# Gated cross-attention kernel: a third stack buffer, whole stacks loaded at once, one merge transfer, a reordered sync queue, and value products of 512 queries in every second slot

## The reference

```python
q, k, v = proj(Wq, bq, norm(x)), proj(Wk, bk, c), proj(Wv, bv, c)   # each 128 x 512
q, k = rope(q, 8), rope(k, 8)                                       # on half of the 16 channels
p = softmax(einsum('bhqd,bhkd->bhqk', q, k) / sqrt(16))             # 8 heads, 512 x 512
x = x + tanh(g_xattn) * (Wo @ einsum('bhqk,bhkd->bhqd', p, v) + bo)
y = (silu(gate) * up) @ w_down ; x = x + tanh(g_ffn) * y / rms(y)   # gate, up = norm(x) @ w_gu
```

## Time and profile before

| what | us |
|---|---|
| median of 3 runs | 921.22 (918.21 to 933.62) |
| the profiled execution | 918.37 |
| its span | 916.6, so 1.8 lie around it |
| mean granted TensorE clock | 0.945 of full speed |
| busy: TensorE, VectorE, ScalarE, GpSimd | 815.8 (89%), 522.1, 483.6, 178.5 |
| first score of batch 0; of batch 1 (step 0) | 39.36; 60.10 |
| stack load of batch 1, first half, issued | 49.77 |
| wait for a stack half in slot 8 of step 0 | 2.0, ends at 76.23 |
| wait of the value group in slot 3 for the copy of pv_sb | 0.23, in nearly every step |
| mix in slot 1, from its start to the value group | 1.05 (224.46 to 225.51) |
| last value group of the attention stage; its last mix | 481.60 to 483.74; 495.13 |
| first instructions of the feed-forward stage | 499.5 |

### The profile page before, as it was taken

How to read it: one execution, slowest core, us unless ns; L and a number is a source line. 1 busy time by engine, 2 the same in 40 slices (tenths; PEclk the granted TensorE clock), 3 DMA queues, 4 the chain that set the end, 5 groups by cost and what they waited for, 6 DMA issues and landing times. The chain is left out here.

```text
span 916.6 us, 13653 instructions
## 1 busy us (share of the span) xinstructions
PE 815.8 (89%) x5110; PEld 421.6 (46%) x5142; DVE 522.1 (57%) x760; ACT 483.6 (53%) x895; POOL 178.5 (19%) x174
## 2 busy tenths in 40 slices
PE   3378999999998988999993599999999999999997
PEld 1123333333333333334332376666666666666664
DVE  4398977888987867888871961314131423141113
ACT  2227776887787766778792552325231623252223
POOL 1232333333333423331112820000000000000000
PEclk8559999999999988999996889999999999999999
DMA  5678555666665666465212010002000110000001
GB/s 167 171 198 218 155 142 153 189 200 194 170 165 152 175 175 189 119 167 153 69 33 79 8 46 1 1 1 67 25 1 1 47 45 0 0 27 21 0 1 46
DMA packets 55176, 86.44 MB, mean 94 GB/s; under 512 B 19274, under 2 KB 20938, under 8 KB 55114
## 3 DMA queue, kind: packets, MB, share of 16 engines
q1 hardware_dynamic: 55114, 85.62, 33.0%
HBM read 44.70 MB, written 34.34 MB: 86 GB/s over the span
## 5 line engine op out<-in xcount | busy, mean ns | idle before, releaser
L670 DVE TENSOR_REDUCE neg_max<-s_ps 128x2 f32<-128x1024 f32 x256 | 310.0, 1219 | 61.8 <-PE s_ps L420 60.8
L536 ACT ACTIVATE probs<-st_ps 128x512 f32<-128x512 f32 x512 | 277.9, 597 | 105.5 <-PE st_ps L432 101.2
L448 PE MATMUL pv_ps<-probs,v_ones 128*32 128x256 f32 x2048 | 166.1, 397 | 12.6 <-ACT pv_sb L542 12.6
L1098 PE MATMUL gu_ps<-x_head,gu_head 128*128 128x512 f32 x352 | 155.9, 443 | 0.0
L965 DVE TENSOR_TENSOR hidden<-gu_ps,silu 128x512 f32<-128x512 f32 x44 | 30.4, 691 | 202.6 <-ACT silu L1040 202.6
L420 PE MATMUL s_ps<-k_stack,q_stack 48*128 48x512 f32 x512 | 135.4, 526 | 10.5 <-DVE neg_max L670 8.4
L1099 PE MATMUL gu_ps<-x_rest,gu_head 128*128 128x512 f32 x352 | 139.0, 395 | 0.0
L1040 ACT ACTIVATE silu<-gu_ps 128x512 f32<-128x512 f32 x44 | 26.3, 597 | 204.8 <-PE gu_ps L1101 204.8
L432 PE MATMUL st_ps<-q_stack,k_stack 50*128 50x512 f32 x512 | 110.6, 421 | 12.9 <-DMA q_stack<-max_scratch 12.7
L420 PEld LDWEIGHTS s_ps<-k_stack,q_stack 48*128 48x128 f32 x512 | 50.4, 193 | 121.1 <-issue 81.1
L1115 PE MATMUL y_ps<-dn_head,h_head 128*128 128x512 f32 x176 | 101.5, 577 | 1.1 <-DVE h_rest L967 1.0
(11 more groups left out here) (114 smaller groups left out, 807.1 us busy)
## 6 DMA issues: line engine op xcount, KB each, us to landing
q_stack<-image SPq DMA_DIRECT2D x64, 192.0 KB, 3.9
k_stack<-image SPq DMA_DIRECT2D x64, 192.0 KB, 4.5
image<-split_head SPq DMA_DIRECT2D x32, 256.0 KB
image<-split_head SPq DMA_DIRECT2D x64, 128.0 KB
image<-split_rest SPq DMA_DIRECT2D x32, 256.0 KB
ct<-ctx_dram SPq DMA_DIRECT2D x16, 256.0 KB, 5.5
swap<-proj SPq DMA_DIRECT2D x64, 64.0 KB, 2.0
scale_of<-inverse_scratch SPq DMA_DIRECT2D x16, 256.0 KB
```

Of the source, the lines that this page charges most:

```text
L448: last = nc.tensor.matmul(pv_ps[2 * KC * j:2 * KC * (j + 1), cols], v_ones[b % 2][:, kt, j, quad, :], probs[at % PROBS][:, j, cols], start ...
L536: nc.scalar.activation(probs[at % PROBS][:, tile % 4, :], st_ps[item % ST_BANKS][:], ACT.Exp).then_inc(st_read, 1)
L670: nc.vector.tensor_reduce(neg_max[j // 2][:, :, j % 2, qt], s_ps[item % S_BANKS][:], AXIS_X, ALU.max, negate=True).then_inc(s_read, 1)
L1098: nc.tensor.matmul(gu_ps[t % 2][:, half], head, x_head[:, k], start=(k == 0), stop=False)
```

## The change

Line numbers of the kernel before are L...; the changed kernel is shorter by 42 lines, so its rows carry other numbers (score products L420 become L405, weight products L432 become L417, value products L448 become L432, mix L456 becomes L439).

1. Three stack buffers instead of two. A stack is loaded whole, four DMAs of 384 KB, at the start of step b for batch b + 2, instead of four of 192 KB for each half, one half at the start of the step and one in its middle.
2. The rotated half is written to `proj` instead of `swap`, and head and rest are each made of both halves at once (128 x 1024): one VectorE cast in slot 11, one GpSimd subtraction. ScalarE's next write to `proj` waits for the rests.
3. The sync queue is reordered, `sync_step` below.
4. `v_ones` and the weights' rows are laid out so that quad 0 has its values on even rows of `pv_sb` and quad 1 on odd ones. The merge is one DMA instead of four, the inverse's store one instead of two, its load two instead of one.
5. A value group is issued whole, 512 queries, in slots 3, 5, ... 15 and in slot 1 of the next step.
6. `values_out` comes ahead of the projection in slot 2. At the start ScalarE does batch 2's projection after the scales and gates.

```diff
-            def load_half(sp, n, h):
-                p = n % 2
-                for w in two:
-                    sp.wait_ge(stored[w], PARTS * (n + 1))
-                if n >= 2:
-                    sp.wait_ge(st_full, last_weight(n - 2, h))
+            def load_stacks(sp, n):
+                sp.wait_ge(stored, PARTS * (n + 1))
+                if n >= STACKS:
+                    sp.wait_ge(st_full, last_weight(n - STACKS, 1))
                 for stack, row0 in ((q_stack, 0), (k_stack, K_ROW0)):
                     for odd in two:
-                        rows = stack[p][STACK * odd:STACK * odd + DATA_ROWS, columns(h), :].bitcast(F32)
-                        heads = slice(odd * PAIRS + 2 * h, odd * PAIRS + 2 * h + 2)
-                        sp.dma_start(rows, image[n, row0:row0 + DATA_ROWS, heads, :]).then_inc(half_in[p][h], 16)
+                        rows = stack[n % STACKS][STACK * odd:STACK * odd + DATA_ROWS, :, :].bitcast(F32)
+                        sp.dma_start(rows, image[n, row0:row0 + DATA_ROWS, odd * PAIRS:(odd + 1) * PAIRS, :]).then_inc(
+                            stack_in[n % STACKS], 16)
...
+            def store_heads(sp, n):
+                sp.wait_ge(heads, n + 1)
+                tile = split_head[:].bitcast(F32)
                 for w in two:
+                    sp.dma_start(image_rows(n, 3 * w + 1, 16), tile[:, w, :]).then_inc(stored, 16)
+                    sp.dma_start(image_rows(n, 3 * w, 8), tile[halves[0], w, :]).then_inc(stored, 16)
+                    sp.dma_start(image_rows(n, K_ROW0 + 3 * w + 2, 8), tile[halves[1], w, :]).then_inc(stored, 16)
...
-                for j in range(QUAD):
-                    rows = slice(2 * KC * j + KC, 2 * KC * (j + 1))
-                    sp.dma_start(pv_sb[0][b % 2][rows, :], pv_sb[1][b % 2][rows, :]).then_inc(merged[b % 2], 16)
+                sp.dma_start(pv_sb[0][b % 2][1:P:2, :], pv_sb[1][b % 2][1:P:2, :]).then_inc(merged[b % 2], 16)
...
             def sync_step(sp, b):
                 nxt, proj_n = b + 1 < B, b + AHEAD_PROJ
-                if nxt:
-                    load_half(sp, b + 1, 1)
+                if b + 2 < B:
+                    load_stacks(sp, b + 2)
                 store_max(sp, b, 1)
+                if b:
+                    gather_sums(sp, b - 1, 1)
                 if proj_n < B:
                     swap_partners(sp, proj_n)
+                load_max(sp, b, 1)
                 if b:
-                    gather_sums(sp, b - 1, 1)
                     merge_quads(sp, b - 1)
-                load_max(sp, b, 1)
                 if b >= 2:
                     store_x(sp, b - 2)
                 if b:
                     store_inverse(sp, b - 1)
-                if proj_n < B:
-                    store_head(sp, proj_n, 1)
-                if b + 2 < B:
-                    load_half(sp, b + 2, 0)
                 if nxt:
                     store_max(sp, b + 1, 0)
+                if b + 5 < B:
+                    load_inputs(sp, b + 5)
                 if b:
                     load_inverse(sp, b - 1)
-                if proj_n < B:
-                    store_rest(sp, proj_n, 1)
-                if b + 5 < B:
-                    load_inputs(sp, b + 5)
                 if nxt:
                     load_max(sp, b + 1, 0)
+                if proj_n < B:
+                    store_heads(sp, proj_n)
                 gather_sums(sp, b, 0)
                 if proj_n < B:
-                    store_head(sp, proj_n, 0)
-                    store_rest(sp, proj_n, 0)
+                    store_rests(sp, proj_n)
...
                 for j in range(QUAD):
-                    last = nc.tensor.matmul(pv_ps[2 * KC * j:2 * KC * (j + 1), cols], v_ones[b % 2][:, kt, j, quad, :],
-                                            probs[at % PROBS][:, j, cols], start=(kt == 0 and part == 0), stop=(kt == KT - 1 and part == 1))
-                if part == 1:
-                    last.then_inc(pv_done, 1)
+                    last = nc.tensor.matmul(pv_ps[2 * KC * j:2 * KC * (j + 1), :], v_ones[b % 2][:, kt, j, 2 * KC * quad:2 * KC * (quad + 1)],
+                                            probs[at % PROBS][:, j, :], start=(kt == 0), stop=(kt == KT - 1))
+                last.then_inc(pv_done, 1)
...
-                    if slot >= 3:
-                        values(pe, b, (slot - 3) // 2, (slot - 3) % 2)
-                    elif slot == 0 and b:
-                        values(pe, b - 1, SPANS - 2, 1)
-                    elif b:
-                        values(pe, b - 1, SPANS - 1, slot - 1)
+                    if slot >= 3 and slot % 2:
+                        values(pe, b, slot // 2 - 1)
+                    elif slot == 1 and b:
+                        values(pe, b - 1, SPANS - 1)
...
-                    if slot == 3 and b:
-                        values_out(act, b - 1, 1)
-                    if slot == 11:
-                        values_out(act, b, 0)
                     for odd in two:
                         exponential(act, b, 2 * slot + odd)
                     if slot == MIX_AT and b >= 2:
                         gate(act, b - 2)
+                    if slot == 2 and b:
+                        values_out(act, b - 1, 1)
+                    if slot == 10:
+                        values_out(act, b, 0)
...
             def swap_partners(sp, n):
                 sp.wait_ge(st_read, ST_NO["rot", n] + 1)
                 if n:
-                    sp.wait_ge(rot_rest, n)
+                    sp.wait_ge(rests, n)
...
-                    if slot == 2:
-                        head_rot(dve, 1)
+                    if slot == 2:
+                        split_heads(dve, 1)
...
-                    if slot == 9:
-                        head_pass(dve, 2)
-                    if slot == 14:
-                        head_rot(dve, 2)
+                    if slot == 13:
+                        split_heads(dve, 2)
```

## The result

| | before | changed |
|---|---|---|
| median | 919.7 us (917.9 to 933.6, 4 runs) | 1008.0 us (1004.0 to 1014.5, 4 runs) |
| ratio, 95% interval | | 1.097 (1.089 to 1.105) |
| span of the profiled execution | 916.6 us | 1007.7 us |
| mean granted clock | 0.945 | 0.887 |
| first V taken in a step | 77.9 us | 90.9 us |

The change makes the kernel 9.7% slower. I had said 938 us, 1.8% slower, with 963 us as the upper end. The direction was right and the size was not: + 13.0 us at the start, + 67.8 in the fourteen steps and + 10.3 behind the last V make the 91.1 us by which the span grew.

The account below looks back on a forecast made before the run. TensorE was taken to bound the attention stage, VectorE close behind. From the profiled 918.4: + 11.5 (fourteen steps) + 4.3 (behind the last V) + 5.3 (start) - 1 (tail) = 938.5, said as 938 us; range 906 to 963.

Parts of the forecast that it names:

- The value order: TensorE in the fourteen steps: whole value groups make a slot pair 2.87 us against 2.48; with the slot-0 wait gone, +11.5.
- The slot-0 wait: TensorE's wait in slot 0 for the next batch's maxima, 12.7 us at nine places, goes, with the slow stretches behind it.
- Step (c): Sync queue, every later step: the burst starts 2.3 us after the slot-0 weight, transfers land in time; cost taken as nothing.
- Rival 4: In the steps: the value order costs as forecast but the slot-0 wait stays, +1.5 x 13, 957 us; chance 0.03.
- Rival 3: Slot 8: maxima late by 1 us or more in 13 steps, +13, clock falls behind four or five, +8; 960 us; chance 0.16.
- Rival 2: TensorE in the steps: 0.4 us idle in each pair lowers the clock once a step, +24, 962 us; chance 0.08.
- the + 4.3 for what is behind the last V: Second half of step 14, +1.6, and step 15, +2.7: slot pairs with whole value groups take longer.
- Rival 1: In the steps: the bank wait is covered, a pair costs 2.35, VectorE sets the step; 878 us; chance 0.10.
- The start: Sync queue before the first step, (a), +2.6 us; together with (b) in step 0, +5.3, bounds 0 and 9.
- (a): Before the first step: batch 2's swap lands behind the burst, first score of step 0 at 62.7 against 60.1, +2.6.
- (b): Step 0: quad 1 maxima come 4.7 us late, 2.0 of it replacing the wait for a stack half; +2.7.
- the tail: Merge and inverse store lose four issues, the inverse load gains one; about -1 us on the chain.

Follow-up runs that it names:

- quad_halves: The changed kernel with stacks loaded by quads again, 0.79 MB at a time, at the two queue places of the kernel before; 940.4 us, ratio 1.013.
- small_first: The changed kernel with the store of quad 1 maxima and the gather of sums issued ahead of the stack loads; 1070.0 us, ratio 1.153.
- late_reciprocal: The changed kernel with VectorE's reciprocal of the sums in slot 10 instead of slot 6; 1040.9 us, ratio 1.125.
- whole_values_old_queue: The kernel before with whole value groups of 512 queries in every second slot; queue, buffers and merge as before; 942.9 us, ratio 1.013.
- half_values_new_queue: The changed kernel with the value products of before, half a group of 256 queries in every slot; 1009.6 us, ratio 1.089.
- quad_halves_half_values: The changed kernel with stacks loaded by quads again and half value groups in every slot; 903.1 us, ratio 0.978 against the kernel before.
- both quads at the head: The changed kernel with stack loads cut into quads, scores waiting for their own quad, both quads issued together at the step's head; 963.5 us, ratio 1.042.
- burst_in_two_places: The changed kernel with query stack loads behind the quad 1 maxima load, key loads behind the next quad 0 maxima load; 961.5 us, ratio 1.032.

## Why the prediction was wrong, point by point

- **The value order** was right in mechanism and size. The pair of slots at 2.87 us measured 2.84 (263.72 to 266.56 below), with the second weight product of the odd slot alone behind a wait for the exponential, and the group of 512 held the line for 0.99 (265.23 to 266.22) where I took 1.01.

```profile
263.72 0.40 PE L417 MATMUL st_ps<-q_stack,k_stack 50*128 50x512 f32 x2
...
264.80 0.50 PE L417 MATMUL st_ps<-q_stack,k_stack 50*128 50x512 f32 x1 [0.22 <-ACT probs L512]
265.23 1.06 PE L432 MATMUL pv_ps<-probs,v_ones 128*32 128x512 f32 x8
266.22 0.50 PE L405 MATMUL s_ps<-k_stack,q_stack 48*128 48x512 f32 x2
266.56 0.40 PE L417 MATMUL st_ps<-q_stack,k_stack 50*128 50x512 f32 x2
```

  The predicted step was 27.8; with the burst undone it was 27.5, and fourteen of them took 382.3 us against the predicted 386.1. In the last batch, without scores, a pair took 2.60 us (554.26 to 556.86) against the predicted 2.63.
- **The slot-0 wait** went, as said: the changed kernel waits once for maxima, 5.7 us in step 0. Rival 4 is out.
- **Step (c) failed**, the overlap of the burst with the steps, which I had put at nothing: "I take nothing for this; it is the thinnest cover of all." It cost 60 us in the fourteen steps, 442.4 against the 382.3 of quad_halves. The burst did begin where I had it (271.86, 2.5 us behind the weight pair of slot 0 at 269.40; I had 2.3). Three other things were wrong. First, I followed only the maxima behind the burst, and they did land in time in the changed kernel. The gather of the sums stands behind the same burst, VectorE's reciprocal in slot 6 is queued on it, and the maxima of the scores on that:

```profile
DVE sums L653 <- DMA sums<-pv_sb: 33.1, 11, 17.6
PE s_ps L393 <- DVE neg_max L636: 13.6, 9, 2.6
```

  In a row of this view stand the wait in all, the number of places and the longest. Of VectorE's 33.1 us, 17.6 are one wait at the very end, so 15.5 lie in front of it at ten places; the second row is TensorE at its V projection. I had named the sums as delayed and then not asked who waits for them; the sentence "VectorE's 21.8 fit in that, with 6 us of slack for its odd jobs" counted work and not order. Second, the burst was mis-sized: 1.57 MB at the 245 GB/s of the earlier trace rows is 6.4 us, and k_stack landed 9.3 us after its issue. That rate was all that the DMA engines moved in that stretch; the page of the kernel before has 4.5 us from issue to landing for half the bytes, which would have given the right size. Third, the clock. The forecast held it at full level; 116 us of the steps ran at the lower one. The waits in themselves were 17.6 us more than in quad_halves, the slower products 42.5. That undoing the burst brings back the 60 us is shown by quad_halves. That the late sums are the path on which it cost them in the changed kernel is read from the trace: the two runs that took this wait away put another in its place (small_first the maxima of slot 8, late_reciprocal those of both slots), so no run prices it alone.
- **Rival 3** was the right kind of thing: late small transfers behind the burst in each step, and the clock behind them. It named the wrong transfer, and its price was 13 + 8 = 21 us where 60 were measured, since it let the clock fall in four or five steps and it was below 1.00 in twelve of fourteen. Its chance of 0.16 was too low, and the range ended at it.
- **Rival 2**, short idles at the banks lowering the clock, is refuted for the full steps: quad_halves and whole_values_old_queue have the idle in each pair and a clock of 1.00 through all fourteen. What the Trainium skill tells of another kernel and I put behind it (TensorE: Matmul & The Clock Gate, A second HAM failure mode: psum-queue depth-cycling) is not seen in these steps. In the last batch, where the scores are gone, it looks like it: TensorE stood 0.45 us in each pair of 2.60 there, against 0.22 in 2.84 in a full step, and the window 562 to 574 above ran at 0.50, with no transfer under way. In the kernel before the same work kept its full clock. So the + 4.3 for what is behind the last V was too small: it was + 8.9 in quad_halves, + 10.3 in the changed kernel and + 13.7 in whole_values_old_queue, and + 0.2 to + 0.3 in the two traces with half groups, half_values_new_queue and quad_halves_half_values.
- **Rival 1**, VectorE as the bound at 878 us, did not come: no full step with whole groups took under 26 us.
- **The start** was said to cost 2.6 and cost 13.0. The mechanism was (a), the swap of batch 2 behind the burst, and its size was off. The burst was issued at 56.31, since it first waits for the landing of the stores, and the swap behind it let GpSimd go at 68.55. I had 49.8 for the burst and 58.2 for the landing. Batch 1's swap stood behind the burst of batch 0 in the same way, which I had not followed (GpSimd went on at 43.16 after 17.74 us of idleness), and the very first scores, which now wait for a whole stack, began at 42.24 instead of 39.36. VectorE then stood 10.06 us at the split and TensorE behind it:

```profile
68.55 1.26 POOL L575 TENSOR_TENSOR swap<-swap,sin 128x512 f32<-128x512 f32 x1 [16.75 <-DMA swap<-proj]
71.31 0.69 DVE L621 CAST split_head<-proj 128x1024 fp32r<-128x1024 f32 x1 [10.06 <-issue]
73.29 0.79 PE L405 MATMUL s_ps<-k_stack,q_stack 48*128 48x512 f32 x2 [11.19 <-DVE neg_max L636]
96.44 0.80 PE L417 MATMUL st_ps<-q_stack,k_stack 50*128 50x512 f32 x2 [5.73 <-DMA q_stack<-max_scratch]
```

- **(b)** measured 5.73 us in slot 8 of step 0, the last of these rows, against 4.7.
- **The rule that transfers are to be coalesced** (the Trainium skill, DMA: Bandwidth & Descriptors, Rules for kernel authors), by which the sum would have been 933, did not decide the time here. Its row speaks of small transfers, under 64 KB above all, and the stack loads had 192 KB before the change. The same bytes in twice as many loads are 68 us faster in quad_halves, at two places of the queue. At one place the number of loads by itself did little: cut in two by rows or by heads the time was 1003 and 999 us against 1008, and only issued quad by quad it was 963. So the runs do not speak against large loads as such. They speak against 1.57 MB at one place of the queue with small transfers behind it.
- **The number 938** came out for the wrong kernel. With the burst undone the traced execution took 940.0 us, and that is partly luck: against before it was + 4.9 at the start, + 7.7 in the fourteen steps and + 8.9 behind the last V, where I had + 5.3, + 11.5 and, with the tail, + 3.3.
- **Two readings** were off without bearing on the sum: in the earlier trace rows the slices below 9 at the start are the first three, and slices 5 to 7 are at 9; and the upper bound of a pair, with a group as dear as two halves, is 2.87 + 0.13 = 3.00, not 2.95.

What stays open: why a wait of one size is followed by the lower clock in one step and not in the next, and how much of the last 35 us between the cut by heads and both quads at the head is the order of issue.

## What to carry to other kernels

When a transfer is made larger, list everything that is issued behind it on the same queue, and for each of these ask which engine's next instruction waits for it and what is queued behind that instruction; slack counted in busy time says nothing about this. A fix for one late transfer must be tried against all others on the queue: at each of the places tried for the long burst something waited for it, at 961 us in the best case and 1070 in the worst. And give a stall on TensorE its price in clock, too: between the changed kernel and quad_halves each microsecond of standing came with 2.4 more of slower products (42.5 against 17.6). That ratio is of this pair; with both quads at the head thirteen steps stood now and then at almost no price in clock.

## What the hardware showed that I had not expected

How fast the burst moved went with the order in which its loads were issued, more than with how it was cut. The lines of the transfers (KB of one, median us to landing), of the changed kernel, where a row brings 8 KB of four heads:

```profile
q_stack<-image SPq DMA_DIRECT2D x32, 384.0 KB, 5.8
k_stack<-image SPq DMA_DIRECT2D x32, 384.0 KB, 9.3
```

and of quad_halves, where it brings 4 KB of two heads:

```profile
q_stack<-image SPq DMA_DIRECT2D x64, 192.0 KB, 3.8
k_stack<-image SPq DMA_DIRECT2D x64, 192.0 KB, 4.5
```

A group of 0.79 MB landed within 4.5 us in quad_halves; in burst_in_two_places the same 0.79 MB as two loads of 384 KB took 5.7 and 6.3 us, at other places of the queue. In nine microseconds from the start of one burst the rates were 166 GB/s with the DMA engines 0.95 busy in the changed kernel, and 200 GB/s at 0.83 with both quads at the head:

```profile
271.90:280.90 9.00, 8.71 (x53) 2.90 (x54) 6.22 (x8) 6.83 (x12) 2.56 (x2) 1.00 0.95 166
```

```profile
196.30:205.30 9.00, 8.72 (x53) 2.89 (x54) 6.23 (x8) 6.85 (x13) 2.57 (x2) 1.00 0.83 200
```

Over all thirteen bursts of a trace, nine microseconds each, the rate was 159 to 178 GB/s in the changed kernel (mean 167, engines 0.93 busy) and 176 to 206 with both quads at the head (mean 193, 0.88). Cut by heads, with the same 4 KB rows and 192 KB loads but all queries issued ahead of all keys, it was 161 to 181 (mean 172, 0.92), and cut by rows 160 to 175 (mean 168, 0.72). So it is not the size of the rows or of the loads that sets these rates apart.

The other surprise is how steep the loss is. Both quads at the head and the cut by heads have the same bytes at the same place, the swap lands 1.3 us apart, and their medians are 963 and 999 us.
